# Routed experts: the shared expert in two parts, groups 0 to 3 ahead of the routed tiles, groups 4 to 7 behind them

## The reference, cut to what matters

```python
h = layernorm(x)
probs = softmax(h @ Wr)                      # 8 experts
topk_vals, topk_idx = top_k(probs, 2)
out = 0
for j in range(7):                           # only the first choice, only experts 0 to 6
    out += 2.0 * topk_vals[0] * swiglu(h, Wu[j], Wg[j], Wd[j]) * (topk_idx[0] == j)
out += swiglu(h, Wu_s, Wg_s, Wd_s)           # the shared expert, for every token
x = x + out
# swiglu(h) = (h @ Wu * silu(h @ Wg)) @ Wd, hidden width 512
```

## Time and profile before

| | us |
|---|---|
| Time, median of 3 executions | 3348.7 |
| The three | 3342.15, 3348.7, 3352.09 |
| The profiled execution: its own time | 3355.69 |
| The profiled execution: its span | 3353.8 |
| Shared expert, routed tiles, gather (of that span) | about 2462 to 2581, 2581 to 2718, 2718 to 2763 |

### The profile page before, as it was taken

The page is one execution under the profiler, slowest core; times in us unless marked ns, Lnnn a source line. Parts: engine busy times, 40 slices in busy tenths (PEclk is TensorE's granted clock), DMA queues, the critical chain, the costliest instruction groups (busy, mean ns, idle before and its releaser), DMA issues. The chain is left out here.

```text
span 3353.8 us, 53186 instructions
## 1 busy us (share of the span) xinstructions
PE 2526.7 (75%) x20516; PEld 1467.6 (44%) x20516; DVE 2096.9 (63%) x4141; ACT 1392.8 (42%) x2771; POOL 607.7 (18%) x581
## 2 busy tenths in 40 slices
PE   5777779999699899978869996788879934334361
PEld 3444546666344344434434444455544622222251
DVE  6888845555687555455545444687752228999657
ACT  5555547776222222222324432378712313444311
POOL 1333421111000233333410000111140030000003
PEclk8888879999799899988979998799979976677665
DMA  1000010000000000010000000200020110000010
GB/s 57 1 2 2 1 35 8 7 7 1 4 1 1 31 2 2 1 46 8 8 4 1 0 1 18 86 8 8 5 69 10 40 40 2 1 0 1 25 53 25
DMA packets 41989, 51.90 MB, mean 15 GB/s; under 512 B 9291, under 2 KB 30869, under 8 KB 40725
## 3 DMA queue, kind: packets, MB, share of 16 engines
q1 hardware_dynamic: 39700, 44.39, 4.2%
q0 software_dynamic: 2048, 4.20, 0.4%
HBM read 39.39 MB, written 9.18 MB: 14 GB/s over the span
## 5 line engine op out<-in xcount | busy, mean ns | idle before, releaser
L130 POOL TENSOR_TENSOR l_rstd<-l_moments,const_minus_half 128x4 f32<-128x4 f32 x104 | 118.6, 1141 | 1570.8 <-DVE l_moments L124 1544.3
L1419 PE MATMUL l_p_gate<-l_h_t,w_wg 128*128 128x512 f32 x400 | 208.4, 603 | 0.0
L1442 PE MATMUL l_p_out<-l_hidden,w_wd 128*128 128x512 f32 x400 | 204.4, 594 | 3.0 <-DVE l_hidden L1712 2.9
L2922 DVE SCALAR_TENSOR_TENSOR l_mix<-l_decay,l_cb 128x1024 f32<-128x1024 f32 x128 | 169.2, 1336 | 45.3 <-ACT l_decay L2805 42.8
L796 DVE TENSOR_REDUCE l_top<-l_ring 128x8 f32<-128x1024 f32 x128 | 150.7, 1220 | 68.0 <-PE l_ring L630 67.6
L2805 ACT ACTIVATE l_decay<-l_p_ring 128x1024 f32<-128x1024 f32 x128 | 130.2, 1031 | 148.2 <-PE l_p_ring L2695 146.8
L348 ACT ACTIVATE l_probs<-l_probs,l_minus_top 128x128 f32<-128x128 f32 x512 | 156.8, 393 | 55.8 <-DVE l_minus_top L407 55.7
L1712 DVE TENSOR_TENSOR l_hidden<-l_act_out,l_p_spread 128x512 f32<-128x512 f32 x128 | 85.7, 685 | 128.9 <-ACT l_act_out L1540 128.7
L3182 PE MATMUL l_p_s<-const_ident,l_z 128*128 128x128 f32 x128 | 29.2, 423 | 179.4 <-ACT l_z L3221 179.4
L1202 DVE TENSOR_REDUCE l_minus_top<-l_p_score 128x4 f32<-128x1024 f32 x64 | 78.2, 1224 | 106.3 <-PE l_p_score L1030 102.5
L136 DVE TENSOR_SCALAR l_h<-x_res,l_moments,l_rstd 128x128 f32<-128x128 f32 (+1 forms) x384 | 112.4, 355 | 44.3 <-POOL l_rstd L130 44.0
(11 more groups left out here) (472 smaller groups left out, 6287.7 us busy)
## 6 DMA issues: line engine op xcount, KB each, us to landing
l_c_t<-in_ctx_t SPq DMA_DIRECT2D x24, 256.0 KB, 2.8
l_rows_in<-l_zero SPq DMA_DIRECT2D x1, 2432.0 KB
l_tile_h<-l_rows_in SPq DMA_DIRECT2D x38, 64.0 KB, 1.9
l_rows_out<-l_tile_y SPq DMA_DIRECT2D x38, 64.0 KB, 1.5
w_mask<-in_mask SPq DMA_DIRECT2D x1, 2048.0 KB, 9.2
w_wg<-in_l2f_wg SPq DMA_DIRECT2D x1, 2048.0 KB
w_wu<-in_l2f_wu SPq DMA_DIRECT2D x1, 2048.0 KB
w_wd<-in_l2f_wd SPq DMA_DIRECT2D x1, 2048.0 KB
```

Source lines behind the costliest of these rows:

```text
L130: return nc.gpsimd.tensor_tensor(rstd[:, :], moments[:, :, 1], minus_half[:, 0:moments.shape[1]], ALU.pow)
L1419: nc.tensor.matmul(p_gate[k % 2][:, :], w["wg"][:, s, :], h_t[:, g % 4, :], start=True, stop=True)\
L1442: nc.tensor.matmul(p_out[:, :], w["wd"][:, s, :], hidden[:, k % 4, :], start=(s == 0), stop=(gated and s == steps - 1)).then_inc(down, 1)
L2922: nc.vector.scalar_tensor_tensor(mix[:, g % RING, :, :], decay[:, g % RING, :, :], 1.0, bcast(cb[:, i % 2, n // 4, :], [T, QH, T], 1), ALU ...
```

## The change

The shared expert becomes a function of a range of groups. Groups 0 to 3 (`FIRST`) run where all eight ran. Groups 4 to 7 (`LAST`) run behind the routed tiles, at the time at which GpSimd gathers. DVE's adds of gathered rows (`add_picked`) are placed between the products of the second part, one group each two steps from the fourth step on; the last two stand at its end. Waits are added where the second part takes over a PSUM or SBUF tile from the routed tiles. The number and kind of all instructions that compute stay the same, GpSimd's and SP's streams are not changed.

```diff
-    LOADS, STORES, GATHERS = 4, 2, 8
+    LOADS, STORES, GATHERS = 4, 2, NG
+    FIRST, LAST = (0, NG // 2), (NG // 2, NG)
...
@@ tensor engine
 shared_up:    +  if s == LAST[0] * CH: pe.wait_ge(tile_hidden, TILES)
 shared_down:  +  if s == LAST[0] * CH: pe.wait_ge(tile_t_ready, TILES)
 turn_back:    +  if j == LAST[0]: pe.wait_ge(hidden_t_ready, TILES)
...
+                def shared(groups):
+                    start, end = groups
+                    shared_up(start * CH)
+                    for s in range(start * CH, end * CH):
+                        if s + 1 < end * CH:
+                            shared_up(s + 1)
+                        if s == 0:
+                            count()
+                        shared_down(s)
+                        if s % CH == 1 and s // CH > start:
+                            turn_back(s // CH - 1)
+                    turn_back(end - 1)
+
+                shared(FIRST)
...
 turn_tile:    -  pe.wait_ge(out_t_ready, NG)
               +  pe.wait_ge(out_t_ready, FIRST[1])
 turn_hidden:  -  pe.wait_ge(added, NG)
               +  pe.wait_ge(added, FIRST[1])
...
+                shared(LAST)
@@ scalar engine: shared(FIRST) ahead of the tiles, shared(LAST) behind them; in it
+                        if s == LAST[0] * CH:
+                            act.wait_ge(tile_hidden, TILES)
@@ vector engine
 shared_hidden: + if s == LAST[0] * CH: dve.wait_ge(hidden_turned, TILES)
-                for s in range(1, NG * CH):
+                for s in range(1, FIRST[1] * CH):
                     shared_hidden(s)
                     if s % CH == 2 and s > CH:
                         add_shared(s // CH - 1)
-                add_shared(NG - 1)
+                add_shared(FIRST[1] - 1)
                 ... the tiles ...
+                def add_picked(g):
+                    dve.wait_ge(gathered[g], 16 * GROUP)
+                    dve.wait_ge(added, g + 1)
+                    for b in range(g * GROUP, (g + 1) * GROUP):
+                        nc.vector.scalar_tensor_tensor(x[:, b, :], picked[:, b, :], weight[:, b:b + 1], x[:, b, :],
+                                                       ALU.mult, ALU.add)
+
+                for n, s in enumerate(range(LAST[0] * CH, LAST[1] * CH)):
+                    shared_hidden(s)
+                    if s % CH == 2 and s // CH > LAST[0]:
+                        add_shared(s // CH - 1)
+                    if n % 2 == 1 and n >= 3:
+                        add_picked((n - 3) // 2)
+                add_shared(NG - 1)
+                add_picked(NG - 1)
```

More of the change, by code:

```diff
@@ L1894, in shared_up @@
                         pe.wait_ge(hidden_ready, s - 1)
+                    if s == LAST[0] * CH:
+                        pe.wait_ge(tile_hidden, TILES)
                     nc.tensor.matmul(p_gate[s % 2][:, :], w["wg"][:, SHARED + c, :], h_t[:, j, :], start=True, stop=True)
@@ L1903, in shared_down @@
                         pe.wait_ge(out_t_ready, j)
+                    if s == LAST[0] * CH:
+                        pe.wait_ge(tile_t_ready, TILES)
                     nc.tensor.matmul(p_turn[0][:, :], w["wd"][:, SHARED + c, :], hidden[:, s % 2, :], start=(c == 0),
@@ L1910, in turn_back @@
                         pe.wait_ge(added, j)
+                    if j == LAST[0]:
+                        pe.wait_ge(hidden_t_ready, TILES)
                     for u in range(GROUP):
@@ L1935, in turn_tile @@
                     else:
-                        pe.wait_ge(out_t_ready, NG)
+                        pe.wait_ge(out_t_ready, FIRST[1])
                     nc.tensor.transpose(p_turn[0][:, 0:T], tile_h[:, t % LOADS, :], const["ident"][:, :]).then_inc(tile_turned, 1)
@@ L1952, in turn_hidden @@
                     else:
-                        pe.wait_ge(added, NG)
+                        pe.wait_ge(added, FIRST[1])
                     for c in range(CH):
@@ L2016, in _, with shared @@
                 route_exp(1)
[L2017 to L2024, removed]
+                def shared(groups):
+                    start, end = groups
+                    for s in range(start * CH, end * CH):
+                        act.wait_ge(gate, s + 1)
+                        if s >= 2:
+                            act.wait_ge(hidden_ready, s - 1)
+                        if s == LAST[0] * CH:
+                            act.wait_ge(tile_hidden, TILES)
+                        nc.scalar.activation(act_out[:, s % 2, :], p_gate[s % 2][:, :], ACT.Silu).then_inc(acted, 1)
+                        if s % CH == 0 and s // CH > start:
+                            copy_out(s // CH - 1)
+                    copy_out(end - 1)
+                shared(FIRST)
                 copy_tile(0)
@@ L2119, in shared_hidden @@
                         dve.wait_ge(down, s - 1)
+                    if s == LAST[0] * CH:
+                        dve.wait_ge(hidden_turned, TILES)
                     nc.vector.tensor_tensor(hidden[:, s % 2, :], act_out[:, s % 2, :], p_up[s % 2][:, :], ALU.mult)\
@@ L2160, in _ @@
                         copy_y(t - 2)
-                for g in range(GATHERS):
-                    dve.wait_ge(gathered[g], 16 * NB // GATHERS)
-                    for b in range(g * NB // GATHERS, (g + 1) * NB // GATHERS):
+                def add_picked(g):
+                    dve.wait_ge(gathered[g], 16 * GROUP)
+                    dve.wait_ge(added, g + 1)
+                    for b in range(g * GROUP, (g + 1) * GROUP):
                         nc.vector.scalar_tensor_tensor(x[:, b, :], picked[:, b, :], weight[:, b:b + 1], x[:, b, :],
                                                        ALU.mult, ALU.add)
+                for n, s in enumerate(range(LAST[0] * CH, LAST[1] * CH)):
[6 more added lines that the diff above has]
+                add_picked(NG - 1)
             @block.gpsimd
```

## The result

Against its own four executions of the kernel before, the change takes the time from 3345.4 to 3309.1 us (medians of four), ratio 0.9893 (95% interval 0.9867 to 0.9918), -36 us. A later comparison (four executions against thirteen of the kernel before) gave 0.9878 (0.9862 to 0.9895), 3339.9 to 3299.4 us, -40.5. But a third one (four against eight) gave 0.9956 (0.9939 to 0.9972), 3355.4 to 3338.6 us, only -17. What separates them is the subject of the experiments.

What follows compares the result with a forecast made beforehand. PE bounds shared expert and tiles; the gather leaves it idle for 45.2 us. Terms -42.9 at the front, +46.7 - 45.2 at the end give -41.4: 3348.7 to 3307.3 us; forecast's own range 3301 to 3314, overall 3301 to 3330.

Steps and rivals of the forecast that it cites:

- Removed from the front: Ahead of the routed tiles: four shared groups of 10.73 us PE time each leave, so the tiles start 42.9 us earlier.
- The tiles move as they are: Routed tiles: all 38 keep their 137.2 us at clock 0.99 and only start earlier.
- The load margin: First tile's load: lands some 15 us before PE needs it; without the front's stalls the price is about 1 us.
- Added at the end: Behind the tiles: second shared part costs 46.7 us with the last picked add, replacing the 45.2 us gather stretch.
- the idle time of 4.1 us: End of step: from DVE's last add at 2763.07 to the next step at 2767.18, put down to the barrier.
- The gather beside it: Beside the second part: gathers at 1.25 us an issue end 2 us early; DVE's 1.14 us adds fit between products.
- Rival 2: Behind the tiles: the gather stretches and sets the end from 1.29 us an issue; at 3.0 us, 3360 us; chance 0.08.
- the rule on the shared port: Gather beside DVE: two-port DVE operations lock GpSimd out, about 3100 ns a DMA against 620; estimated time 3363 us.
- the prediction's own formula: Gather's end is 2677.7 + 31 i + 2.4 + 1.1 for an issue distance i.
- Rival 1: Beside the gather: the 16.7 us stall seen beside the scatter comes once more; gain 24.7 us, time 3324; chance 0.32.

Runs made afterwards that it cites:

- experiments 2 to 7: The changed kernel again; three or five groups behind the tiles; gathered adds behind the second part; no gather, in the changed kernel and the one before; ratios 0.9869 to 0.9981.
- experiment 2: The changed kernel run again without any edit, against the kernel before: ratio 0.9878, step time 257.7 us, no stall.
- experiment 1: The kernel before run again without any edit: ratio 0.9995, step time 295.7 us, no stall.
- Experiment 5: Changed kernel with all eight adds of gathered rows put behind the second part: ratio 0.9981 to the kernel before, step time 306.4 us.
- 8: Changed kernel with the two counting matmuls behind step 0's calls, so row numbers come earlier: ratio 0.9948 to the kernel before, step time 306.6 us.
- 9: The changed kernel a third time, without any edit, against the kernel before: ratio 0.9956, step time 299.0 us.
- 12: Changed kernel with the counting matmuls (row numbers) earlier, run once more in the third group: ratio 0.9963 to the kernel before, step time 303.5 us.
- the first group: The first four follow-up runs, together on one chip: both kernels again, three and five groups behind the tiles; kernel before 3339.9 us.
- experiment 6: Changed kernel without the 32 gathers and DVE's adds of their rows: ratio 0.9873 to the kernel before, step time 275.7 us.
- 10: Changed kernel with each gather replaced by a plain DMA of 128 consecutive rows from GpSimd's queue: ratio 0.9886 to the kernel before, step time 269.7 us.
- 11: Changed kernel with each gather replaced by a plain DMA of the same bytes from SP's queue: ratio 0.9885 to the kernel before, step time 277.3 us.

## Why the prediction was right, point by point

The forecast was 3307 us and -41.4 us; measured were 3309.1 us and -36 us, in the forecast's own range of 3301 to 3314. The mechanism, work moved beside the gather and hidden there, is shown (experiments 2 to 7). That the first measurement came so near is in part luck, told at the end of this list.

- **Removed from the front, 42.9 us.** Measured 42.4 without stalls on either side, 40.2 with one on both (112.4 to 72.2).
- **The tiles move as they are.** Not quite: 133.8 to 138.1 us in the pair without stalls. In experiment 2 the granted clock was 0.50 from 2524 to 2528, behind short waits of PE for a load and for copies, while in experiment 1 it stayed at 1.00 over its first tiles. The fifth tile is turned 12.0 us behind the first instead of 9.3, 2.7 of the 4.3 us. The rest stays open: the same stage varied from 133.7 to 142.3 us over all runs. The prediction had put this term at nothing. It outweighs the 1.4 us by which the end (below) was priced too high.
- **The load margin.** 15 us in the stalled profile, next to nothing without the stall, as the prediction had said; PE's wait was a few tenths of a us.
- **Added at the end, 46.7 - 45.2 = +1.5 us.** Measured 0.1 without stalls. The shared work took what was worked out (DVE's last add of shared rows ended 45.6 us behind the first gate call), but GpSimd ends the step in both kernels, 7.69 us behind its last issue. The term was mis-sized since the idle time of 4.1 us ahead of the next step was read as the barrier's. With a stall the same term is +26 us.
- **The gather beside it.** Issue distances of 1.26 us on average (39.16 / 31 after, against 1.25 before), no wait of DVE for gathered rows ahead of a product, the adds hidden. Experiment 5 shows the other side, +7.1 us when they are not.
- **Rival 2 and the rule on the shared port.** Falls: beside PE, ACT and DVE at work GpSimd's issue distance was 1.26 us on average, 1.40 us for the longest single one (1.30 in the kernel before). The Trainium skill (SBUF — State Buffer, "SBUF: two separate sides") gives about 3100 ns for a DMA under a two-port DVE operation. Nothing like that is seen here with DVE's products and weighted adds. By the prediction's own formula the gather would have set the end from 1.31 us on, not from 1.29; the difference decides nothing.
- **Rival 1.** The mechanism is real, and it had 0.32. In the two groups that stall beside the scatter, every kernel with the second part and the gather (5, 8, 9, 12) stalls beside the gather too. It was priced at 16.7 us from the front. That sum counts one call too many: between the starts at 2500.71 and 2528.14 lie 11 calls, 9.9 us of work, so 17.6 us were lost, and the two fronts of the kernel before differ by 17.7. Beside the gather the stall costs 25.9. There the change brings 17 us, not 24.7, and the time, 3338.6 us, lies beyond the rival's 3336. What the prediction did not see is that the stall went with the group of runs rather than the kernel: none of the four profiles of the first group stalled beside the scatter, all four of the second did and all four of the third, with the kernel before at 3339.9, 3360.6 and 3355.4 us. Each group had its own chip and its own time, so that the runs can't say which of the two it goes with. The two profiles of the first comparison held one of each kind. So its -36 us fell near the forecast by luck: it is neither the change without stalls, 38 to 41 us, nor the change with them, 17.

## What to carry to other kernels

Work that waits for nothing in the stretch can be moved beside a transfer that leaves the engines idle, and pays up to the shorter of the two. The split is right where both bounds are level, here four groups of eight, with one group either way costing 7 to 9 us without stalls. Before believing a gain worked out from one profile, profile the kernel before once more, on another chip if possible, and compare the changed step between marks of its own: untouched steps drifted by 16 us here, and a stall of 18 to 26 us came and went from one group of runs to the next. And ask of the last stage which engine's stream really ends last; an idle time ahead of the next step need not be the barrier's.

## What the runs showed of the hardware that was not expected

Beside GpSimd's indirect DMAs, ACT and DVE got PE's results up to 23 us behind the end of PE's records in two groups of runs, with 18 to 20 us lost in all beside the scatter and 26 beside the gather; nothing was late in the other group, the changed kernel among it. Beside the gather it is gone when the indirect DMAs are left out (experiment 6, one profile), and with plain DMAs of the same bytes (10 and 11, with their shorter exposure). The scatter was never left out, and plain DMAs were never stretched over 39 us, so it is not shown that it takes an indirect DMA. Whether PE itself ran late, with records that give its starts and only modelled ends, or whether its semaphore events were held up, the profile can't tell, nor why one group has it and another not; this stays open. The Trainium skill (SBUF — State Buffer, "SBUF: two separate sides") holds that engine ports and DMA ports can't contend. No run here shows a port to be the cause, but the runs do show compute held up while indirect DMAs run. GpSimd, when its stream ends with indirect DMAs, let the next step start 7.69 us after its last issue, against 1.0 to 1.5 us after DVE's last instruction when DVE is last.
